# First and last steps of a shifted-window transformer block in another order, with transposes that TensorE makes while it waits

## The reference

```python
h = layernorm(x) * g1 + b1
h = roll(h, (-3, -3), axis=(1, 2))                  # shifted windows of 7 x 7
xw = windows(h)                                      # [32 * 64, 49, 128]
q, k, v = split(xw @ w_qkv + b_qkv)                  # 4 heads of 32
attn = (q * 32 ** -0.5) @ k.T + bias(rel_table) + mask
out = softmax(attn) @ v @ w_proj + b_proj
x = x + roll(unwindow(out), (3, 3), axis=(1, 2))
h2 = layernorm(x) * g2 + b2
y = x + gelu(h2 @ w_fc1 + b_fc1) @ w_fc2 + b_fc2     # 128 -> 512 -> 128
```

## Time and profile before

| | |
|---|---|
| median of 3 runs | 2950.26 us (2950.23 to 2952.65) |
| profiled execution, its own time | 2950.09 us |
| its span | 2948.1 us |
| PE busy | 2908.3 us, 99% of the span |
| DVE busy | 2647.9 us, 90% |
| ACT busy | 2305.5 us, 78% |
| POOL busy | 1326.5 us, 45% |

### The profile page before, as it was taken

How to read it: one execution, slowest core, us unless ns; L and a number is a source line. 1 busy time by engine, 2 the same in 40 slices (tenths; PEclk the granted TensorE clock), 3 DMA queues, 4 the chain that set the end, 5 groups by cost and what they waited for, 6 DMA issues and landing times.

```text
span 2948.1 us, 120004 instructions
## 1 busy us (share of the span) xinstructions
PE 2908.3 (99%) x52240; PEld 2745.7 (93%) x52240; DVE 2647.9 (90%) x7590; ACT 2305.5 (78%) x4606; POOL 1326.5 (45%) x776
## 2 busy tenths in 40 slices
PE   6999999999999999999999999999999999999999
PEld 5999999999999999999999999999999999999998
DVE  7999999999999999899999999999999999999985
ACT  4778787878787777777877877787878787878785
POOL 3444444444444444444444444444444444444442
PEclk9999999999999999999999999999999999999999
DMA  2111111111111111111111111111111111111111
GB/s 58 35 35 41 35 41 38 38 35 41 40 36 37 40 41 35 38 38 41 36 40 36 41 35 41 35 41 35 41 37 39 35 41 39 38 35 41 39 26 23
DMA packets 217597, 111.82 MB, mean 38 GB/s; under 512 B 15118, under 2 KB 216814, under 8 KB 217070
## 3 DMA queue, kind: packets, MB, share of 16 engines
q1 hardware_dynamic: 214675, 103.16, 13.8%
q10 hardware_dynamic: 2395, 1.00, 0.2%
HBM read 52.73 MB, written 51.38 MB: 35 GB/s over the span
## 4 chain that ended last, share of the span: by engine, by line
PE 98%; ACT 1%; DVE 1%; issue 0%; SPq 0%; DMA 0%; ACTq 0%
PE psum L1484 26%; PE psum L1444 11%; PE psum L1446 9%; PE psum L1445 9%; PE psum L1412 8%; PE psum L1463 8%; PE psum L1427 7%; PE psum L1470 7%; PE psum L1419 6%; PE psum L1439 6%; DMA brow_proj_in<-in_b_proj 0%; ACT hT L504 0%; ACT qd L491 0%; SPq L275 0%; ACT oT L467 0%
## 5 line engine op out<-in xcount | busy, mean ns | idle before, releaser
L1484 PE MATMUL psum<-wfc,hT 128*112 128x128 f32 x7168 | 804.4, 273 | 0.7 <-ACT hT L504 0.7
L322 POOL TENSOR_TENSOR probs<-probs,row_inv 128x784 f32<-128x784 f32 x256 | 414.8, 1621 | 843.9 <-DVE row_inv L1024 843.9
L1484 PEld LDWEIGHTS psum<-wfc,hT 128*112 128x112 f32 x7168 | 790.0, 177 | 1.3 <-ACT hT L504 1.2
L326 POOL TENSOR_TENSOR rstd<-ve,minus_half 112x7 f32<-112x7 f32 x256 | 380.5, 1486 | 754.5 <-DVE ve L990 754.5
L504 ACT ACTIVATE hT<-psum,bias_h 128x392 f32<-128x392 f32 x1024 | 568.4, 592 | 43.9 <-PE psum L1446 42.3
L491 ACT ACTIVATE qd<-psum,bias_q,parity_one 128x392 f32<-128x392 f32 x512 | 322.6, 686 | 270.1 <-PE psum L1446 270.1
L1029 DVE TENSOR_TENSOR stream<-psum,stream 112x512 f32<-112x512 f32 (+1 forms) x512 | 316.8, 619 | 133.1 <-PE psum L1484 78.2
L1444 PE MATMUL psum<-x2T_hi,wfc_hi 128*128 128x392 f32 x1024 | 389.4, 380 | 2.1 <-DVE x2T_lo L1040 1.0
L1446 PE MATMUL psum<-x2T_lo,wfc_hi 128*128 128x392 f32 x1024 | 348.9, 341 | 0.7 <-issue 0.7
L1445 PE MATMUL psum<-x2T_hi,wfc_lo 128*128 128x392 f32 x1024 | 347.6, 339 | 0.0
L1010 DVE TENSOR_TENSOR psum<-psum,bias_rel 128x784 f32<-128x784 f32 x256 | 250.6, 979 | 83.9 <-PE psum L1412 83.9
(11 more groups left out here) (76 smaller groups left out, 5844.5 us busy)
## 6 DMA issues: line engine op xcount, KB each, us to landing
x_in<-in_x SPq DMA_DIRECT2D x224, 168.0 KB
out<-stream SPq DMA_DIRECT2D x223, 168.0 KB
x_in<-in_x SPq DMA_DIRECT2D x224, 17.5 KB
out<-stream SPq DMA_DIRECT2D x223, 17.5 KB
x_in<-in_x SPq DMA_DIRECT2D x224, 10.5 KB
out<-stream SPq DMA_DIRECT2D x223, 10.5 KB
x_in<-in_x SPq DMA_DIRECT2D x32, 96.0 KB
out<-stream SPq DMA_DIRECT2D x32, 96.0 KB
```

Of the source, the lines that this page charges most:

```text
L322: pool.tensor_tensor(p, p, r.unsqueeze(2).to_broadcast([128, 2 * WINDOWS, N]), ALU.mult).then_inc(probs_normed[band], 1)
L326: pool.tensor_tensor(rstd[:, :], ve[:, :], minus_half[:, :], ALU.pow).then_inc(ready, 1)
L1484: last = pe.matmul(tok_psum(h)[0:TOK, (t - t0) * C:(t - t0 + 1) * C], hT[:, chunk, t * TOK:(t + 1) * TOK], wfc2[:, chunk, :], start=chunk ...
```

## The change

It writes the head and the tail of each engine's program in another order. The computation is the same, but for transposes of the identity into a PSUM bank that nobody reads yet (`keep_warm`). The loop bodies of DVE, ACT and POOL are the same; PE's loop has one more wait. The diff is long (some 1600 lines, nearly all of them calls that change places); this is its core.

```diff
             load(0, 0)
-            sp.dma_start(mask_sb[:, :, :, :], mask).then_inc(mask_loaded, 16)
-            load_rel(sp, 0)
             load(0, 1)
             for dst, src in ((wproj[:, :], w_proj), (brow_proj_in[:, :], b_proj.to_broadcast([TOK, C]))):
                 sp.dma_start(dst, src).then_inc(proj_loaded, 16)
+            sp.dma_start(mask_sb[:, :, :, :], mask).then_inc(mask_loaded, 16)
+            load_rel(sp, 0)
             for s in range(2, STEPS):
                 load(0, s)
...
             pool.wait_ge(x_loaded[(0) % STEPS], dma_count((0) % STEPS, (0) // STEPS))
+            pool.wait_ge(brow_ready, 1)
             add_row(0, x_in, brow_proj, x_biased)
             pool.wait_ge(x_loaded[(1) % STEPS], dma_count((1) % STEPS, (1) // STEPS))
             add_row(1, x_in, brow_proj, x_biased)
+            pool.wait_ge(x_loaded[(2) % STEPS], dma_count((2) % STEPS, (2) // STEPS))
+            add_row(2, x_in, brow_proj, x_biased)
             pool.wait_ge(inv_ready[0], 1)
             normalise_probs(0)
...
+            act.wait_ge(xT_made[1], 1)
+            copy_x(0, 1)
             act.wait_ge(xT_made[0], 1)
             copy_x(0, 0)
-            copy_x(0, 1)
-            act.wait_ge(xT_copied[1], 1)
+            act.wait_ge(xT_copied[0], 1)
             round_x(0, 0)
             round_x(0, 1)
...
             normalise(xn1, x_in[:, (0) % STEPS, :, :], mean1, rstd1, xn1_ready, 1)
+            normalise(xn1, x_in[:, (0) % STEPS, :, :], mean1, rstd1, xn1_ready, 0)
             scale_qkv()
-            normalise(xn1, x_in[:, (0) % STEPS, :, :], mean1, rstd1, xn1_ready, 0)
             dve.wait_ge(wqk_rounded, 1)
             split_qk_weights()
             dve.wait_ge(x_loaded[(1) % STEPS], dma_count((1) % STEPS, (1) // STEPS))
             stats1(1)
-            dve.wait_ge(bias_h_products, 1)
-            make_late_biases()
+            dve.wait_ge(xT_rounded[0], 1)
+            split_x(0, 0)
+            dve.wait_ge(xT_rounded[1], 1)
+            split_x(0, 1)
             dve.wait_ge(raw1_done, 2)
             mean_var(raw1, part1, mean1, ve1, raw1_done, parts1_done, stats1_done, var1_ready, upto(1))
-            dve.wait_ge(xT_rounded[0], 1)
-            split_x(0, 0)
             dve.wait_ge(x_loaded[(2) % STEPS], dma_count((2) % STEPS, (2) // STEPS))
             stats1(2)
...
+            def keep_warm(count):
+                for _ in range(count):
+                    pe.transpose(psum[:, QKVO_BANK, 0:128], ident[:, :], ident[:, :])
+
+            pe.wait_ge(ident_ready, 1)
+            keep_warm(24)
             pe.wait_ge(cleared, 1)
             pe.wait_ge(xT_cleared, 1)
-            pe.wait_ge(ident_ready, 1)
 
             make_qkv_biases()
+            keep_warm(14)
             pe.wait_ge(xn1_ready[1], 1)
             transpose_tiles(xn1, 1, xT_made)
-            make_proj_bias()
-            make_hidden_biases()
             pe.wait_ge(xn1_ready[0], 1)
             transpose_tiles(xn1, 0, xT_made)
+            keep_warm(18)
             pe.wait_ge(xT_split[0], 1)
+            make_q(0, 0)
             make_k(0, 0)
-            make_q(0, 0)
...
                 make_out(0)
+                pe.wait_ge(v_copied[0], n + 1)
                 pe.wait_ge(xT_split[0], n + 2)
                 make_q(n + 1, 0)
...
             pe.wait_ge(gelu_done[7], steps)
+            make_out(0)
             make_out(1)
-            make_out(0)
```

More of the change, by code:

```diff
@@ L791, in _ @@
             copy_x2(1)
-            act.wait_ge(x2T_made[0], steps - 3)
-            copy_x2(0)
+            act.wait_ge(fc1_made[0], steps - 3)
+            gelu(0)
             copy_probsT(steps - 3, 0)
-            copy_k(0)
             copy_probsT(steps - 3, 1)
@@ L798, in _ @@
             gelu(1)
-            gelu(0)
-            act.wait_ge(o_made[0], steps - 2)
-            copy_o(1)
+            act.wait_ge(fc1_made[2], steps - 3)
+            gelu(2)
+            act.wait_ge(o_made[1], steps - 2)
             copy_o(0)
@@ L838, in _ @@
+            copy_k(0)
+            copy_probsT(steps - 2, 0)
             act.wait_ge(x2T_made[1], steps - 2)
             copy_x2(1)
-            copy_probsT(steps - 2, 0)
+            act.wait_ge(o_made[0], steps - 1)
+            copy_o(0)
+            copy_o(1)
+            gelu(0)
             act.wait_ge(fc1_made[1], steps - 2)
             gelu(1)
-            gelu(0)
+            act.wait_ge(q_made[1], steps)
+            copy_q(1)
+            act.wait_ge(fc1_made[2], steps - 2)
+            gelu(2)
@@ L858, in _ @@
-            gelu(6)
+            act.wait_ge(fc1_made[4], steps - 2)
+            gelu(4)
             act.wait_ge(fc1_made[7], steps - 2)
             gelu(7)
-            act.wait_ge(fc1_made[4], steps - 2)
-            gelu(4)
+            act.wait_ge(scores_shifted[0], steps)
             exp(0)
+            act.wait_ge(v_made[0], steps)
+            copy_v()
+            act.wait_ge(x2T_made[0], steps - 1)
+            copy_x2(0)
             act.wait_ge(scores_shifted[1], steps)
             exp(1)
-            act.wait_ge(gelu_loaded, steps - 1)
@@ L867, in _ @@
-            load_gelu_table()
-            act.wait_ge(x2T_made[0], steps - 1)
-            copy_x2(0)
-            copy_v()
             act.wait_ge(x2T_made[1], steps - 1)
@@ L1117, in _ @@
             split_x2(0)
-            dve.wait_ge(x2T_copied[1], 1)
-            split_x2(1)
-            dve.wait_ge(scores_made[0], 3)
-            shift_scores(2, 0)
-            mean_var(raw1, part1, mean1, ve1, raw1_done, parts1_done, stats1_done, var1_ready, upto(3))
+            copy_v()
+            normalise(xn2, stream[:, (0) % STEPS, :, :], mean2, rstd2, xn2_ready, 1)
             split_x(2, 1)
@@ L1145, in _ @@
             mean_var(raw2, part2, mean2, ve2, raw2_done, parts2_done, stats2_done, var2_ready, upto(1))
-            copy_v()
+            dve.wait_ge(scores_made[1], 3)
+            shift_scores(2, 1)
+            dve.wait_ge(rstd2_ready, 2)
+            normalise(xn2, stream[:, (1) % STEPS, :, :], mean2, rstd2, xn2_ready, 1)
+            dve.wait_ge(exp_done[0], 3)
+            inverse_sums(2, 0)
+            dve.wait_ge(xT_rounded[0], 4)
+            split_x(3, 0)
+            inverse_sums(2, 1)
@@ L1169, in _ @@
+            dve.wait_ge(residual_added[1], 3)
             stats2(2)
-            dve.wait_ge(v_made[1], 4)
-            copy_v()
             dve.wait_ge(raw2_done, 3)
@@ L1295, in _ @@
             normalise(xn2, stream[:, (steps - 4) % STEPS, :, :], mean2, rstd2, xn2_ready, 0)
+            dve.wait_ge(v_made[1], steps - 2)
+            copy_v()
+            dve.wait_ge(fc2_made[0], steps - 4)
+            add_to_stream(steps - 5, 0, out_added)
             dve.wait_ge(exp_done[0], steps - 2)
@@ L1352, in _ @@
-            dve.wait_ge(residual_added[1], steps - 1)
+            dve.wait_ge(residual_added[0], steps - 1)
             stats2(steps - 2)
+            dve.wait_ge(raw2_done, steps - 1)
+            mean_var(raw2, part2, mean2, ve2, raw2_done, parts2_done, stats2_done, var2_ready, upto(steps - 2))
+            shift_scores(steps - 1, 0)
             dve.wait_ge(v_made[1], steps)
             copy_v()
-            dve.wait_ge(raw2_done, steps - 1)
-            mean_var(raw2, part2, mean2, ve2, raw2_done, parts2_done, stats2_done, var2_ready, upto(steps - 2))
@@ L1358, in _ @@
-            dve.wait_ge(scores_made[1], steps)
-            shift_scores(steps - 1, 1)
             dve.wait_ge(rstd2_ready, steps - 1)
@@ L1784, in _ @@
             make_k(steps - 3, 0)
-            pe.wait_ge(out_added[1], steps - 5)
-            transpose_tiles(xn2, 1, x2T_made)
             pe.wait_ge(out_added[0], steps - 5)
@@ L1790, in _ @@
             transpose_probs(0)
+            pe.wait_ge(xn2_ready[1], steps - 4)
+            transpose_tiles(xn2, 1, x2T_made)
             pe.wait_ge(q_copied[0], steps - 2)
```

816 lines of the change are left out of this document (398 added, 418 removed).

## The result

The changed kernel took 2943.28 us (median of 9 runs, 2937.34 to 2944.8), the kernel before 2951.39 (9 runs, 2948.44 to 2953.18). The ratio is 0.9973, with a 95% interval from 0.9965 to 0.9982: faster by 0.27%, with 2942.5 predicted. The profiled execution took 2942.71 us, its span is 2940.8.

What follows compares the result with a forecast made beforehand. PE was taken to bound the loop (busy 2908.3 of 2948.1 us), so the gain had to come from the head. 7.4 + 1.3 - 1.1 = 7.6 us less than 2950.1 gave 2942.5, range 2939.8 to 2945.4.

Steps and rivals of the forecast that it cites:

- The first q and the first scores: Head: PE starts q at 16.2 in place of 21.70, `shift_scores` at 22.9 in place of 29.96, 7.1 us earlier.
- rival B: Head: transposes don't raise the clock, q starts at 17.6, `shift_scores` at 25.5, lead 2.6 us less, 2945.1 us; chance 0.22.
- The step that named DVE, not PE, as the engine that ends this stretch: Head, up to the first scores: DVE's work ends at 22.9, PE's scores are ready at 22.4 and hidden.
- Tokens loaded ahead of the mask ... zero both ways: Head, SP's loads: earlier step 1 tokens gain nothing, and the mask queued behind them costs nothing; zero.
- Lead at xn2: Head, transposes of `xn2` at 58.98 before: they come 7.4 us earlier.
- the idle time of DVE's chain: Head, DVE's work up to `xn2`: idle 1.8 us in the new order, where it was 2.2.
- From there to 76.30: Head behind the `xn2` transposes: PE regains 1.3 of 2.1 us lost to idling and the lowered clock.
- From 76.30 to the loop: Last stretch of the head: PE idles 0.49 in 44.65 us, so nothing to gain; 0.
- The added wait: PE's loop: one more met wait per turn costs 0; upper bound 10.8 us.
- The end: Last stores: six DMAs per queue behind the last addition in place of three; last one lands 1.1 us later.
- The tail's other moves ... zero, by 0.7 either way: Tail: other moves touch waits of 0.2 to 0.5 us each; zero, by 0.7 us either way.
- The rule against the warm-up: Head: the skill says transposes don't count as busy for the clock; the sum assumed they raise it; by the rule, 2945.1.

Runs made afterwards that it cites:

- e10: Changed kernel with its 56 extra transposes of 128 columns replaced by 56 of 8 columns, all at the first group's place: 2942.06 us, ratio 0.9978.
- e6b: Kernel before with one part alone: projection and hidden biases behind the first k and q, DVE's late biases behind `make_bias_rel`: 2945.16 us, ratio 0.9981.
- e3: Changed kernel with the DMAs of mask and relative biases ahead of step 1's tokens again: 2942.45 us, ratio 0.9977.
- e4: Changed kernel with the loop's added wait written four times in a row instead of once: 2945.62 us, ratio 0.9992.
- e2: Changed kernel with the last stores in the order of the additions, half 0 first on SP and ACT: 2939.87 us, ratio 0.9972.
- e9: Changed kernel's head and loop with the tail of the kernel before, on all engines: 2938.48 us, ratio 0.9966.
- e11b: Changed kernel, its 56 transposes moved (16 ahead of first q, 32 and 8 in two later waits), last stores in addition order; repeated for a profile: 2938.49 us, ratio 0.9959.
- e1: Changed kernel without its 56 extra transposes of `ident`: 2948.48 us, ratio to the kernel before 1.0002.
- e7: Changed kernel with 32 and 8 more transposes of `ident` in two more of PE's waits in the head: 2939.57 us, ratio 0.9974.
- e12: Changed kernel with 40 transposes of 8 columns ahead of its first 24, 96 extra ones in all: 2947.45 us, ratio 0.9991.

## Why the prediction held, step by step

**The first q and the first scores.** q was forecast for 16.2 and came at 17.40. The sum took the clock as raised by then, but the 18 transposes ahead of q ran at the low one (0.21 us each, granted clock 0.52 from 13.85 to 17.40) and held PE, as rival B had it; the rest `xT_lo` was made from 16.01 on. It cost nothing, since the products behind them ran at the high clock. `shift_scores` came at 23.10 for 22.9, and counted from the tokens it is 0.3 earlier than forecast. The step that named DVE, not PE, as the engine that ends this stretch was right, as long as those products are fast: at the low clock (e10) DVE waits 1.19 us for PE there. POOL just fits, as said (0.24 us).

**"Tokens loaded ahead of the mask ... zero both ways"** is open. The statistics of step 1 did not wait in the kernel before and in e6b; with the same DMA order e3 waited 0.94 us. The new order is worth between nothing and about 1 us.

**Lead at xn2: 7.4** forecast, 6.1 measured, 6.6 without the landing. The term that was off is the idle time of DVE's chain, put at 1.8 us: from 23.10 to 51.70 DVE is idle for 3.1 (28.60 less 25.51), of which it waits 1.80 for 14 projections that take 2.92 us at the low clock.

**From there to 76.30: 1.3** forecast, 1.8 measured (15.52 for 17.32), with the clock at 1.00. **From 76.30 to the loop** I had 0; it is 0.9. Together the head gives 8.8 for 8.7: three terms were off by 0.5 to 1.3 us and cancelled, and that they did is luck.

**The added wait: 0**, right within the noise of the loop, by e4.

**The end: 1.1** was right as a mechanism and a little small: the stores cost 1.3 (e2). **"The tail's other moves ... zero, by 0.7 either way"** was the weakest term: the new tail loses another 0.7 (e9), at the edge of what I allowed. The noise of the loop, 0.9 in favour, hid it in the profile.

**The rule against the warm-up.** Rival B took the clock as the thing at stake. Transposes of `ident` did raise it here: 0.22 us each in the first group, 0.12 in the second, and the bias products behind them took 0.80 us for 1.41 without (e11b). So the rule of the Trainium skill ("TensorE: Matmul & The Clock Gate", Part 4: PE-mode transpose) that transpose mode doesn't count as busy for the clock disagrees with this trace, and the measurement decides. But B's price of 2.6 us was wrong as well: e10, at the low clock up to the first scores, loses 1.4 there and 0.3 at the loop. Neither side of my comparison saw what the 56 transposes do for the time: they shift the code behind them, and at that place PE doesn't stop. Without them the change would have been worth nothing (e1), so the forecast was right with one cause missing from it, and that this place is a good one is luck, too.

**What stays open.** The stops go with the place of the code: in six profiles of five kernels with the new tail, 56 transposes and the loop as it is there is none above 0.5 us behind 2820, and the four kernels with 0 or 96, or with three waits more in the loop, have two each. What PE lacks there is most likely its next instructions, by the packets of q8, but no run tests that alone. Nor is it settled why the clock of one and the same head is low for 6.8 us between 29.00 and 48.00 in the changed kernel's two executions (granted clock 0.82 over these 19 us), for 10.3 in e9 (0.73) and for 17.1 in e4 (0.55).

## What to carry to other kernels

Find the engine that ends the stretch and count a lead from where its chain starts to where another engine takes over: 3 us at the first scores became 0.2 at the loop (e6b), and 1.4 lost there became 0.3 (e10). When an edit adds or removes instructions in code that runs once, look far behind it for stops that nothing releases, and keep the count with filler before the edit's own effect is read. Compare the stops with the instruction packets of the trace. Put a warm-up into the wait just ahead of the stretch that ran at the low clock (2.3 us in e7, where the one placed earlier gave 0.3 at most), and store the last results in the order in which they are made.

## What the hardware showed that I had not expected

- PE stops of 1.2 to 2.2 us with all its inputs there, in code that runs once, present or absent with the number of instructions ahead. In the loop they were at most 0.66 us. All 54 stops of 0.3 us or more end 2.3 to 3.0 us behind the start of a 16 KiB packet on the instruction queue q8.
- After some such stops (e1 at 83.44, both of e4), as after a wait of 1.1 us (41.06), PE ran at the lower of its two levels, 1.2 GHz, for some us: 14 projections took 2.92 us there, for 1.78 at 2.4 GHz. After the stops of e7 and e12 it did not, nor after the same wait in e10 (42.68).
- 119 turns of the loop, which differs by at most four waits between the kernels, took 2684.67 to 2690.71 us, and in two executions of one kernel 2689.86 and 2687.97; the first tokens landed at 6.79 to 7.47.
